# Moving the first chunk of x from TensorE transposes to a VectorE transpose through memory, with a later `fade` and new orders

## The chip, the cores and the metric

One of the cores of a Trainium2 chip runs the whole program. The time is the device time of one execution in microseconds, given as the median of several runs.

## The reference, cut to what matters

One layer works on an input of 2 sequences of 512 tokens and 512 channels: a layer norm, a state-space scan with a convolution, gates and a grouped norm, a product back to 512 channels, and then a feed-forward block with low-rank additions. What the change touches is the scan and the data it reads.

```python
proj = input_states @ in_proj_w.T             # gate, xBC, dt
xBC = silu(causal_conv(xBC, taps=4) + conv_b)  # x: 128 heads x 64; B, C: 8 groups x 128
cum = cumsum(dt * A)                           # within a chunk
scores = (C @ B.T) * exp(cum_i - cum_j), masked to j <= i
y_intra = scores @ (dt * x)                    # inside a chunk
state   = exp(cum_last) * state + B.T @ (dt * exp(cum_last - cum) * x)
y_inter = (C * exp(cum)) @ state_before        # across chunks
y = y_intra + y_inter + D * x
g = rmsnorm_by_group(y * silu(gate)) * norm_w
out = x_in + g @ out_w.T                       # then the feed-forward block
```

The result does not depend on the length of a chunk; the kernel uses chunks of 128 tokens.

## The kernel before

**Tiling.** The 128 heads come in 8 groups of 16 heads. A group has 1024 channels of x (8 tiles of 128) and one tile each of B and C. Each of the 2 sequences has `SC` = 4 chunks of 128 tokens, so that a group has 8 slots, `k` = 0 to 7, with `b = k // 4` the sequence and `c = k % 4` the place in it. `K = 8 g + k` numbers all 64 slots. All products are made with fp32 values split into a high and a low part (`_h`, `_l`): three matmuls for one product.

**What a slot does.** While slot `k` works on its chunk, the projections of the unit after it (group and sequence) run between: 18 weight tiles, 5 in each of the first three slots of a sequence and 3 in the last one (`SLOT_TILES`). Tile names are `g` for a gate tile and `c` for a convolved tile. PE's order in a slot is: `inside` (line 1899, the chunk's own scores times `xdt`), `square_total` (1976), `new_state` (lines 1821 to 1823 on `xw_h`, `xw_l`, `b_tok_h`, `b_tok_l`), one tile, `turn_x` (1873) where the next chunk is turned on PE, `match` (1882, 1883) and `across` (1914) of the next chunk, and the rest of the tiles with the two halves of the out-projection (`out_half`, lines 1960, 1943, 1950) between them. In a sequence's last slot there is no `new_state` and no `across`.

**Turning x.** The convolved x lies with channels on partitions (`x_ch`), and `xdt` and `xw` need tokens there. For `c` = 0, and for the first three slots of all, PE does eight 128x128 transposes into the banks `xt`, from which DVE multiplies by dt (`scale_x`, line 1481). For the other chunks DVE transposes blocks of 32x32 (`turn_x`, line 1503) into a staging buffer, SP stores that in four pieces to memory (`store_x`, line 530), fetches it back as rows (`fetch_x`, line 540, into `x_rows`), and DVE scales it from there (line 1490). `x_sq_of` and `on_pe` say which chunk goes which way.

**The other engines' steps.** DVE adds the skip term (`add_skip`, 1533), moves or adds the new state (`add_state`, 1572 and 1570), reads the mean square (1578), multiplies by the gate (`gated`, 1546), adds to the output (`accumulate`, 1584), decays the state (`fade`, 1555), convolves (`taps`, 1458), scales `across` (1522), makes the low part of the output weights (`ow_low`, 1464, in a group's first slot) and multiplies the scores (`scores`, 1512). POOL makes the low parts of the weights (`w_low`, 771), masks (`mask`, 777), makes `xw` (`weigh_x`, 796) and `xw_l` (`xw_low`, 804) and `gT_l` (`gT_low`, 811), and sums squares (817 to 821). ACT makes the high parts, drains banks and takes the exponentials (1026). `inside` needs `xdt_ready` and the slot's scores, `new_state` needs `xw_l`.

**Buffers share memory.** `under` places a name on the memory of the next one. `x_rows` lies on `gT_l`, `xw` and `xw_sq` on `xw_l`, `ec_sq` on `ec`. So `gT_low` of a slot has to wait until `scale_x` of the next chunk has read `x_rows`.

**What sets the order.** Each engine runs its own list of instructions in the order written out by hand in `body(g, last)`, once for every engine, and waits on semaphores. All DMAs go through one queue, issued by SP in its written order; a wait on SP holds every DMA behind it.

## Time and profile before

| what | value |
|---|---|
| median of 3 runs | 1715.68 us (1715.34 to 1719.24) |
| profiled execution | 1716.82 us, its span 1715.0 us |
| PE busy | 1696.1 us, 99% |
| DVE, POOL, ACT busy | 1298.6, 1229.7, 1194.9 us |
| granted TensorE clock | 0.999 of full speed |
| `turn_x` on PE, line 1873 | 144 transposes, 14.4 us busy |
| fetches of x, line 540 | 46 of 512 KB |

The groups 1 to 6 repeat each other: PE's idle time before a group's first slot's fifth tile, for one, comes every 184.8 us. So one boundary between two groups, from 614 to 662 us, is read in detail. A timeline merges equal instructions that follow each other; a busy time in it is that of the merged row. A matmul of 512 columns starts 0.23 us after the one before it, although its row says 0.39: they overlap.

### The profile page before, as it was taken

The page shows a single profiled execution, that of the slowest core. Times are in us where ns is not written, and L with a number is a line of the kernel's source. Part 1 is how long each engine was busy: PE and PEld are TensorE (multiplying, and loading weights), DVE is VectorE, ACT ScalarE, POOL GpSimd, SP SyncE. Part 2 cuts the span into 40 slices and gives each one's busy share as a digit, 9 for nine tenths or more (in the row PEclk, how much of TensorE's full clock was granted, in tenths as well). Part 3 has the DMA queues.
Part 4 walks back from the last instruction along what each step waited for, and adds up shares of the span by engine and source line. Part 5 has one row for each costly group of instructions (what it writes and reads, how often), then busy time and mean ns, then how long its engine had stood idle before and what let it go on. Part 6 is the DMA issues. An engine that isn't in the chain of part 4 may idle for free.

```text
span 1715.0 us, 27399 instructions
## 1 busy us (share of the span) xinstructions
PE 1696.1 (99%) x9557; PEld 1406.3 (82%) x9557; DVE 1298.6 (76%) x2200; ACT 1194.9 (70%) x2232; POOL 1229.7 (72%) x1058
## 2 busy tenths in 40 slices
PE   9999999999999999999999999999999999999999
PEld 7788888888888888888888888888888888787887
DVE  8897778868796879787986889687977799664323
ACT  6877677777877787777777777768777777663411
POOL 5586778787787778787877788777878687774610
PEclk9999999999999999999999999999999999999999
DMA  5654547464665555555746465556555564554301
GB/s 188 175 137 140 166 145 214 118 172 134 201 166 152 160 170 159 151 155 148 213 131 168 117 203 163 152 164 184 164 147 148 154 201 117 164 137 136 86 10 49
DMA packets 155176, 259.86 MB, mean 152 GB/s; under 512 B 27936, under 2 KB 56224, under 8 KB 155040
## 3 DMA queue, kind: packets, MB, share of 16 engines
q1 hardware_dynamic: 155040, 258.11, 52.4%
q8 instruction: 77, 1.26, 0.3%
q14 instruction: 59, 0.48, 0.1%
HBM read 229.21 MB, written 28.84 MB: 150 GB/s over the span
## 4 chain that ended last, share of the span: by engine, by line
PE 90%; DVE 5%; POOL 1%; issue 1%; DMA 1%; ACT 1%; SPq 0%; DVEq 0%; ACTq 0%; POOLq 0%
PE bank L1821 18%; PE bank L1823 17%; PE bank L1822 17%; PE bank L1899 7%; PE bank L1960 6%; PE bank L1943 6%; PE bank L1950 6%; PE bank L1914 4%; DVE ow_l L1464 2%; PE bank L2204 1%; PE bank L2206 1%; PE bank L2205 1%; PE bank L1976 1%; DVE bcT L1458 1%; PE bank L1883 1%
## 5 line engine op out<-in xcount | busy, mean ns | idle before, releaser
L771 POOL TENSOR_TENSOR w_l<-w_raw,w_h 128x512 fp32r<-128x512 f32 x288 | 397.6, 1383 | 270.2 <-ACT w_h L973 269.9
L1821 PE MATMUL bank<-x_h,w_h 128*128 128x512 f32 (+1 forms) x1328 | 527.1, 397 | 10.0 <-DVE bcT L1458 5.9
L1823 PE MATMUL bank<-x_h,w_l 128*128 128x512 f32 (+1 forms) x1328 | 519.1, 391 | 0.0
L1822 PE MATMUL bank<-x_l,w_h 128*128 128x512 f32 (+1 forms) x1328 | 518.1, 390 | 0.0
L1026 ACT ACTIVATE decay<-decay,cols 128x128 f32<-128x128 f32 x1024 | 318.3, 390 | 3.6 <-POOL decay L777 1.5
L1458 DVE SCALAR_TENSOR_TENSOR x_ch<-bank,par,x_ch 128x511 f32<-128x511 f32 (+2 forms) x384 | 286.3, 746 | 34.2 <-ACT x_ch L991 25.0
L1821 PEld LDWEIGHTS bank<-x_h,w_h 128*128 128x128 f32 (+1 forms) x1328 | 249.6, 188 | 64.1 <-issue 11.7
L1823 PEld LDWEIGHTS bank<-x_h,w_l 128*128 128x128 f32 (+1 forms) x1328 | 249.1, 188 | 54.0
L1822 PEld LDWEIGHTS bank<-x_l,w_h 128*128 128x128 f32 (+1 forms) x1328 | 249.8, 188 | 50.5
L777 POOL TENSOR_SCALAR_AFFINE_SELECT decay<-decay 128x512 f32<-128x512 f32 x256 | 200.7, 801 | 69.6 <-DMA decay<-cum_scratch 68.6
L1512 DVE TENSOR_TENSOR decay<-decay,bank 128x512 f32<-128x512 f32 x256 | 171.0, 682 | 81.6 <-ACT decay L1026 81.4
L991 ACT ACTIVATE x_ch<-bank,par 128x512 f32<-128x512 f32 x128 | 98.9, 773 | 154.6 <-PE bank L1823 154.6
L1533 DVE SCALAR_TENSOR_TENSOR bank<-x_ch,par,bank 128x128 f32<-128x128 f32 x512 | 138.3, 349 | 81.7 <-PE bank L1899 81.7
L973 ACT ACTIVATE w_h<-w_raw 128x512 fp32r<-128x512 f32 x288 | 178.9, 622 | 15.2 <-DMA w_raw<-in_wp 15.1
L811 POOL TENSOR_TENSOR gT_l<-sgT,gT_h 128x1024 fp32r<-128x1024 f32 x64 | 154.1, 2407 | 8.4 <-DVE xdt L1490 7.6
L1012 ACT ACTIVATE sgT<-bank 128x512 f32<-128x512 f32 x122 | 71.8, 590 | 102.9 <-PE bank L1823 102.7
L1960 PE MATMUL bank<-ow_h,gT_h 128*128 128x512 f32 x512 | 137.3, 390 | 0.0
L1943 PE MATMUL bank<-ow_l,gT_h 128*128 128x512 f32 x512 | 136.9, 389 | 0.0
L1950 PE MATMUL bank<-ow_h,gT_l 128*128 128x512 f32 x512 | 136.8, 389 | 0.0
L1899 PEld LDWEIGHTS bank<-decay,xdt 128*64 128x64 f32 x2048 | 110.5, 137 | 22.6 <-issue 22.6
L1899 PE MATMUL bank<-decay,xdt 128*64 128x128 f32 x2048 | 125.9, 276 | 0.0
L804 POOL TENSOR_TENSOR xw_l<-xw,xw_h 128x1024 fp32r<-128x1024 f32 x48 | 115.0, 2396 | 0.3 <-ACT xw_h L1038 0.3
(164 smaller groups left out, 2775.8 us busy)
## 6 DMA issues: line engine op xcount, KB each, us to landing
w_raw<-in_wp SPq DMA_DIRECT2D x288, 256.0 KB, 3.6
decay<-cum_scratch SPq DMA_DIRECT2D x256, 256.0 KB, 4.7
ec<-ecum_scratch SPq DMA_DIRECT2D x96, 256.0 KB, 7.0
x_rows<-xt_scratch SPq DMA_DIRECT2D x46, 512.0 KB, 3.3
ow_raw<-in_ow SPq DMA_DIRECT2D x64, 256.0 KB, 5.4
xt_scratch<-xw_sq SPq DMA_DIRECT2D x124, 128.0 KB, 3.0
w_raw<-in_w SPq DMA_DIRECT2D x48, 256.0 KB, 2.8
xt_scratch<-ec_sq SPq DMA_DIRECT2D x60, 128.0 KB, 2.4
```

Of the source, the lines that this page charges most:

```text
L771: pool.tensor_tensor(w_l[:, s, :], w_raw[:, s, :], w_h[:, s, :].bitcast(F32), ALU.subtract).then_inc(wl_ready, 1)
L777: pool.affine_select(out=d, in_=d, compare_op=ALU.is_ge, fill=fill, base=0, pattern=[[0, QH], [1, P]], channel_multiplier=-1).then_inc(mas ...
L973: act.activation(w_h[:, s, :], w_raw[:, s, :], ACT.Copy).then_inc(wh_ready, 1)
L1026: last = act.activation(decay[:, h, :], decay[:, h, :], ACT.Exp, bias=cols[:, b, CUM, c, h:h + 1], scale=-1.0)
L1458: dve.scalar_tensor_tensor(out=conv(bu, t)[:, s:], in0=bank_of(u, i)[:, 0:SEQ - s], scalar=w, in1=conv(bu, t)[:, s:], op0=ALU.mult, op1=AL ...
L1821: pe.matmul(dst, wh, xh, start=(opens and k == 0), stop=False)
L1822: pe.matmul(dst, wh, xl, start=False, stop=False)
L1823: last = pe.matmul(dst, wl, xh, start=False, stop=(k == len(terms) - 1 and not more))
L1899: last = pe.matmul(yb[n // 4][a * HDIM:(a + 1) * HDIM, tok(n % 4)], xdt[:, h * HDIM:(h + 1) * HDIM], decay[:, h, :], start=(c == 0), stop= ...
L1943: last = pe.matmul(ob[:, :], gT_h[:, n, :], ow_l[:, n, :], start=False, stop=(k == 0 and n == CT - 1))
L1950: last = pe.matmul(ob[:, :], gT_l[:, n, :], ow_h[:, n, :], start=False, stop=(k > 0 and n == CT - 1))
L1960: pe.matmul(ob[:, :], gT_h[:, n, :], ow_h[:, n, :], start=(n == 0), stop=False)
```

## The change

What it does, engine by engine:

- All first chunks but the very first (`K` = 4, 8, ..., 60; 15 of them) are turned by DVE into `gT_sq`, a new name on the memory of `gT_l`, stored, and fetched into `xw`. PE's `turn_x` remains for `K` = 0, 1, 2. Chunks `c` = 2 are staged in `xh_sq`, a new name on `xw_h`. The scratch memory and its semaphores become four (`SC`) in place of two, and the counts in `moved_no` and `stored_no` follow.
- DVE, last slot of a sequence: `turn_x` of the next first chunk directly behind `add_skip`; `accumulate`, `turn_x` of its second chunk and three of the four `scores` ahead of `scale_x`.
- DVE, first slot of a sequence: `mean_square` and `gated` ahead of `add_state`. First slot of a group: `fade` behind the taps of its third tile.
- PE, first slot of a sequence (but the very first): its first tile ahead of `new_state`, its second behind.
- SP, last slot: `store_x` and `fetch_x` of the first chunk ahead of the store of the third.
- POOL, last slot: `gT_low` waits for the store of the first chunk; `square_sum` ahead of `weigh_x`.
- ACT, last slot: all exponentials and both remaining tiles ahead of `xw_high`; in a sequence's first slot `xw_high` waits for the store out of `xh_sq`.
- The last group's second sequence gets matching orders, and a few waits of PE name other semaphores (left out below).

```diff
@@ -461,19 +463,19 @@
-            return ec_sq if k % SC == 1 else xw_sq
+            return (gT_sq, ec_sq, xh_sq, xw_sq)[k % SC]
+
+        def rows_at(k):
+
+            return xw if k % SC == 0 else x_rows
         def on_pe(K):
-            return K % SC == 0 or K < SC - 1
-
-        def pe_no(K):
-
-            return K + 1 if K < SC - 1 else SC - 1 + K // SC
+            return K < SC - 1
         def moved_no(K):
-            return 1 if K < SC else (SC - 1) * (K // SC - 1) + K % SC + 1
+            return K - SC + 2
...
@@ -525,19 +527,20 @@
                 sp.wait_ge(x_turned, turned_no(K))
-                dst = xt_dram[K % 2].rearrange("(b t) (c f) -> c t b f", b=QUADS, c=QUADS)
+                dst = xt_dram[K % SC].rearrange("(b t) (c f) -> c t b f", b=QUADS, c=QUADS)
                 for q in range(QUADS):
                     sp.dma_start(dst[q], x_sq_of(k)[q * SQ:(q + 1) * SQ, :, :, :].rearrange("p b n t -> p b (n t)")
-                                 ).then_inc(x_stored[K % 2], 16)
+                                 ).then_inc(x_stored[K % SC], 16)
             def fetch_x(g, k):
                 K = g * CHUNKS + k
                 if on_pe(K):
                     return
-                sp.wait_ge(x_stored[K % 2], stored_no(K))
-                sp.wait_ge(out_done, 2 * (K - 1))
-                sp.dma_start(x_rows[:, :], xt_dram[K % 2]).then_inc(x_fetched, 16)
+                sp.wait_ge(x_stored[K % SC], stored_no(K))
+                if k % SC > 0:
+                    sp.wait_ge(out_done, 2 * (K - 1))
+                sp.dma_start(rows_at(k)[:, :], xt_dram[K % SC]).then_inc(x_fetched, 16)
...
@@ -717,6 +720,8 @@
                     if c == SC - 1:
+                        store_x(gn, kn)
+                        fetch_x(gn, kn)
                         store_x(gn, kn + 2)
...
@@ -790,9 +795,7 @@
                 if c == 2:
-                    pool.wait_ge(x_stored[1], stored_no(K + 1))
-                elif c == 0 and some(K):
-                    pool.wait_ge(x_stored[0], stored_no(K + 2))
+                    pool.wait_ge(x_stored[SC - 1], stored_no(K + 1))
                 pool.tensor_tensor(per_head(xw[:, :]), per_head(xdt[:, :]), spread(cols[:, b, ELAST, c, :], HDIM),
...
@@ -806,7 +809,9 @@
                 pool.wait_ge(gTh_ready, K + 1)
-                if not on_pe(K + 1):
+                if c == SC - 1 and K < GROUPS * CHUNKS - 1:
+                    pool.wait_ge(x_stored[0], stored_no(K + 1))
+                elif K < GROUPS * CHUNKS - 1 and not on_pe(K + 1):
                     pool.wait_ge(xdt_ready, K + 2)
...
@@ -937,8 +942,11 @@
                         norm_inverse(1, 1)
+                    if c == SC - 1:
+                        square_sum(g, k)
                     weigh_x(gn, kn)
-                    square_sum(g, k)
+                    if c < SC - 1:
+                        square_sum(g, k)
                     if c == SC - 1:
...
@@ -1035,6 +1043,9 @@
                 act.wait_ge(xw_ready, n_state(g, k) + 1)
+                K = g * CHUNKS + k
+                if k % SC == 0 and some(K):
+                    act.wait_ge(x_stored[2], stored_no(K + 2))
                 act.activation(xw_h[:, :], xw[:, :], ACT.Copy).then_inc(xw_h_ready, 1)
...
@@ -1272,13 +1283,11 @@
                         for q in range(QUARTERS):
-                            if q == QUARTERS - 1 and not last:
-                                xw_high(gn, kn)
                             exps(gn, kn, q)
                         if last:
-                            xw_high(gn, kn)
                             norm_high(1, 2)
                         tile(tiles[1:-1] if last else tiles[1:])
+                        xw_high(gn, kn)
                         if k == CHUNKS - 1:
...
@@ -1494,6 +1503,8 @@
                 dve.wait_ge(silu_done, conv_no(2 * g + b, CONV_TILES))
+                if c == 0:
+                    dve.wait_ge(out_done, 2 * (K - 1))
                 if c == 1:
...
@@ -1662,9 +1673,9 @@
                     add_skip(LAST, k)
-                    add_state(LAST, k)
                     norm_apply(1, k - 1)
                     gated(LAST, k)
+                    add_state(LAST, k)
                     norm_low(1, k - 1)
...
@@ -1730,10 +1741,16 @@
                     add_skip(g, k)
+                    if c == SC - 1:
+                        turn_x(gn, kn)
                     if first:
                         gated(g, k)
                         add_state(g, k)
                         taps_of(tiles[2:3])
+                    elif c == 0:
+                        mean_square(*before)
+                        gated(g, k)
+                        add_state(g, k)
                     else:
...
@@ -1761,11 +1778,14 @@
                             ow_low(g, j)
+                    if c == SC - 1:
+                        accumulate(*before)
+                        turn_x(gn, kn + 1)
+                        for q in range(QUARTERS - 1):
+                            scores(gn, kn, q)
                     scale_x(gn, kn)
-                    if not first:
+                    if not first and c < SC - 1:
                         accumulate(*before)
-                    if c == SC - 1:
-                        turn_x(gn, kn + 1)
                     if k == 0:
...
@@ -1775,21 +1795,23 @@
                     taps_of(tiles[1:2])
-                    if k == 0 and not first:
-                        fade(gn, kn)
                     if k > 0:
                         scale_across(gn, kn)
-                        scores(gn, kn, 0)
-                        scores(gn, kn, 1)
+                        if c < SC - 1:
+                            scores(gn, kn, 0)
+                            scores(gn, kn, 1)
                     if not first:
                         taps_of(tiles[2:3])
                     if k == 0:
+                        if not first:
+                            fade(gn, kn)
                         scale_across(gn, kn)
                         for j in range(OW_EARLY + 2, CT):
                             ow_low(g, j)
                         scores(gn, kn, 0)
                         scores(gn, kn, 1)
-                    scores(gn, kn, 2)
+                    if c < SC - 1:
+                        scores(gn, kn, 2)
                     if k == 0:
...
@@ -2076,9 +2096,10 @@
                     square_total(LAST, k - 1)
+                if k == SC:
+                    project(LAST, 1, TILES - 1)
                 new_state(LAST, k)
                 if k == SC:
-                    project(LAST, 1, TILES - 1)
                     match(LAST, k + 1)
...
@@ -2140,10 +2161,15 @@
                         square_total(*((g, k - 1) if k else (g - 1, CHUNKS - 1)))
+                    late_state = c == 0 and not first
+                    if late_state:
+                        projects(tiles[:1])
                     new_state(g, k)
                     if first:
                         projects(tiles[3:4])
-                    if not first:
+                    if late_state:
+                        projects(tiles[1:2])
+                    elif not first:
                         if last and c == SC - 1:
...
@@ -2167,7 +2192,7 @@
                     if not first:
-                        projects(tiles[1:3])
+                        projects(tiles[2 if c == 0 else 1:3])
                     out_half(g, k, 0)
```

## Rows read from the trace of the kernel before

**Rows 1.** Page, first part: busy time of every engine, share of the span.

```profile
PE 1696.1 (99%) x9557; PEld 1406.3 (82%) x9557; DVE 1298.6 (76%) x2200; ACT 1194.9 (70%) x2232; POOL 1229.7 (72%) x1058
```

**Rows 2.** Waits of PE: waiting line, releaser: us in total, times, longest.

```profile
PE bank L1821 <- DVE bcT L1458: 5.9, 7, 0.9
```

**Rows 3.** Timeline (start us, us, operation, [idle before]): PE, sequence's last slot, transposes.

```profile
619.66 0.40 PE L1823 MATMUL bank<-x_h,w_l 128*128 128x512 f32 x1
619.89 0.80 PE L1873 MATMUL bank<-ident_r,x_chr 128*128 128x128 f32 x8
620.53 0.25 PE L1882 MATMUL bank<-ident_r,bcTr 128*128 128x128 f32 x1
```

**Rows 4.** Timeline of PE: out-projection of that slot, then the group's first slot.

```profile
626.39 1.07 PE L1960 MATMUL bank<-ow_h,gT_h 128*128 128x512 f32 x4
...
631.92 1.97 PE L1899 MATMUL bank<-decay,xdt 128*64 128x128 f32 x32
...
634.06 0.48 PE L1821 MATMUL bank<-xw_h,b_tok_h 128*128 128x512 f32 x1
...
652.25 0.47 PE L1821 MATMUL bank<-x_h,w_h 128*128 128x512 f32 x1 [0.80 <-DVE bcT L1458]
...
660.05 0.48 PE L1821 MATMUL bank<-xw_h,b_tok_h 128*128 128x512 f32 x1
```

**Rows 5.** Timeline of SP: the four stores of a chunk of `x` in that slot.

```profile
620.71 1.76 SPq L530 DMA_DIRECT2D xt_scratch<-xw_sq  x4
```

**Rows 6.** Source view of line 530, the stores: issue to landing.

```profile
DMA to landing us min/median/max: 2.0/2.9/5.5
```

**Rows 7.** Source view of line 540, the fetches: issue to landing.

```profile
DMA to landing us min/median/max: 3.1/3.3/6.8
```

**Rows 8.** Timeline of POOL over both slots.

```profile
624.26 2.41 POOL L811 TENSOR_TENSOR gT_l<-sgT,gT_h 128x1024 fp32r<-128x1024 f32 x1
626.63 1.91 POOL L796 TENSOR_TENSOR xw<-xdt,cols 128x1024 f32<-128x1024 f32 x1
...
633.43 2.56 POOL L771 TENSOR_TENSOR w_l<-w_raw,w_h 128x512 fp32r<-128x512 f32 x2
639.67 1.28 POOL L771 TENSOR_TENSOR w_l<-w_raw,w_h 128x512 fp32r<-128x512 f32 x1 [3.68 <-ACT w_h L973]
...
642.24 2.40 POOL L811 TENSOR_TENSOR gT_l<-sgT,gT_h 128x1024 fp32r<-128x1024 f32 x1 [0.34 <-DVE xdt L1490]
644.59 4.21 POOL L777 TENSOR_SCALAR_AFFINE_SELECT decay<-decay 128x512 f32<-128x512 f32 x4
...
657.39 2.38 POOL L804 TENSOR_TENSOR xw_l<-xw,xw_h 128x1024 fp32r<-128x1024 f32 x1
```

**Rows 9.** Timeline of DVE over both slots.

```profile
616.04 2.16 DVE L1533 SCALAR_TENSOR_TENSOR bank<-x_ch,par,bank 128x128 f32<-128x128 f32 x8 [2.75 <-PE bank L1899]
...
628.24 0.69 DVE L1512 TENSOR_TENSOR decay<-decay,bank 128x512 f32<-128x512 f32 x1 [0.49 <-ACT decay L1026]
...
635.74 1.29 DVE L1572 COPY state<-bank 128x512 f32<-128x512 f32 x2 [0.51 <-PE bank L1823]
637.01 1.28 DVE L1546 TENSOR_TENSOR sgT<-bank,sgT 128x512 f32<-128x512 f32 x2
638.20 1.41 DVE L1464 SCALAR_TENSOR_TENSOR ow_l<-ow_raw,par,ow_h 128x512 fp32r<-128x512 f32 x2
640.05 2.05 DVE L1490 TENSOR_TENSOR xdt<-x_rows,cols 128x512 f32<-128x512 f32 x2 [0.44 <-DMA x_rows<-xt_scratch]
642.68 5.63 DVE L1464 SCALAR_TENSOR_TENSOR ow_l<-ow_raw,par,ow_h 128x512 fp32r<-128x512 f32 x4
648.23 1.65 DVE L1555 TENSOR_TENSOR state<-state,cdec 128x1024 f32<-128x1024 f32 x1
649.80 2.31 DVE L1458 SCALAR_TENSOR_TENSOR bcT<-bank,par,bcT 128x511 f32<-128x511 f32 x3
...
655.97 2.47 DVE L1512 TENSOR_TENSOR decay<-decay,bank 128x512 f32<-128x512 f32 x4
```

More of the change, by code:

```diff
@@ L131, in build @@
     cols_dram = nc.dram_tensor("cols_scratch", (GROUPS, BATCH, P, UNIT_COLS), F32, kind="Internal").ap()
-    xt_dram = nc.dram_tensor("xt_scratch", (2, P, GCH), F32, kind="Internal").ap()
+    xt_dram = nc.dram_tensor("xt_scratch", (SC, P, GCH), F32, kind="Internal").ap()
     cdec_dram = nc.dram_tensor("cdec_scratch", (BATCH, GROUPS, GH * SC), F32, kind="Internal").ap()
@@ L180, in build @@
         xdt = sc("xdt", [P, GCH])
+        xh_sq = under("xh_sq", [P, QUADS, CT, SQ])
         xw_h = sc("xw_h", [P, GCH], F32R)
@@ L189, in build @@
         x_rows = under("x_rows", [P, GCH])
+        gT_sq = under("gT_sq", [P, QUADS, CT, SQ])
         gT_l = sc("gT_l", [P, CT, P], F32R)
@@ L334, in build @@
         x_turned = sem("x_turned")
-        x_stored = [sem(f"x_stored{n}") for n in range(2)]
+        x_stored = [sem(f"x_stored{n}") for n in range(SC)]
         x_fetched = sem("x_fetched")
@@ L482, in stored_no @@
         def stored_no(K):
-            return 16 * QUADS * (K // 2 if K % 2 else K // SC)
+            return 16 * QUADS * (K + 1) // SC if K % SC == SC - 1 else 16 * QUADS * (K // SC)
         @block.sync
@@ L1471, in scale_x @@
                 if on_pe(K):
-                    dve.wait_ge(tx_done, pe_no(K))
+                    dve.wait_ge(tx_done, K + 1)
                 else:
@@ L1484, in scale_x @@
                     return
-                xs = x_rows.rearrange("p (a s n t) -> p a n s t", a=2, s=QUADS // 2, n=CT)
+                xs = rows_at(k).rearrange("p (a s n t) -> p a n s t", a=2, s=QUADS // 2, n=CT)
                 xd = xdt.rearrange("p (n a s t) -> p a n s t", n=CT, a=2, s=QUADS // 2)
@@ L1830, in norm_transpose @@
                 if k == 1 and c == 2:
-                    pe.wait_ge(xdt_ready, (GROUPS - 1) * CHUNKS + SC + 1)
+                    pe.wait_ge(x_l_ready, CHUNKS + 1)
                 if k == 1 and c in (SC, SC + 1):
@@ L1866, in turn_x @@
                     pe.wait_ge(silu_done, conv_no(2 * g + b, CONV_TILES))
-                if K == MIDDLE + 1:
-                    pe.wait_ge(x_l_ready, CHUNKS + 2)
                 if some(K):
@@ L1974, in square_total @@
                 if K == MIDDLE:
-                    pe.wait_ge(xdt_ready, K + 2)
+                    pe.wait_ge(x_l_ready, CHUNKS + 2)
                 pe.matmul(total_of(K), y[:, 0, :], ones[:, :], start=True, stop=True).then_inc(ss_done, 1)
@@ L2153, in body @@
                         projects(tiles[1:-1])
-                        turn_x(gn, kn)
                     else:
```

## Prediction

> **What bounds the kernel now.** I read the busy times first. PE is busy for 1696.1 us of a span of 1715.0 [rows 1], so only two things move the time: work taken from PE, and waits given to it. The waits of PE come next. The only one that repeats is 5.9 us in 7 pieces, PE behind the taps of the tile `bcT` [rows 2], once in each group's first slot (groups 1 to 7). The timeline of one boundary between groups then shows how near the other engines are to PE. In the group's first slot DVE has work in every microsecond from 640.05 to the last scores at 658.4 [rows 9], and POOL's last piece, `xw_l`, ends at 659.77 [rows 8] for a `new_state` at 660.05 [rows 4]. That is 0.28 us to spare on POOL. So this slot is bound by three engines at once, while a sequence's last slot is bound by PE alone.
>
> **Eight transposes go, 15 times.** Without them the product `match` would start where the first transpose starts: 620.53 - 619.89 = 0.64 us [rows 3]. 15 x 0.64 = 9.6 us off PE. For the boundary into the last group's second sequence I count it separately below; 14 x 0.64 = 9.0 us for the others. This step is sure, as nothing else runs on PE in that time.
>
> **What replaces them in the last slot.** DVE transposes when `add_skip` ends, at 618.20 [rows 9]. SP now issues its first store of this slot at 620.71, as soon as DVE has turned that chunk [rows 5]; the new chunk is turned earlier, and I take 620.45 for its first store. The fourth is issued 1.3 us later and lands 2.9 us after that [rows 6]: 624.7. Two things hang on it.
> First, `gT_l`. POOL started it at 624.26 [rows 8]; it would start at 624.7 and end at 627.1. The out-projection starts 0.64 us earlier than 626.39 [rows 4], and its third set of four matmuls (0.91 us a set, four starts 0.23 apart as in [rows 3]) needs `gT_l` at 625.75 + 1.81 = 627.56. Cover 0.45 us, cost nothing; with a landing at the longest 5.5 us [rows 6] it would cost 2.1.
> Second, the fetch: 624.75 + 3.3 [rows 7] = 628.1. `scale_x` now stands behind the third `scores`, which ends at 628.93 [rows 9], so the fetch is hidden by 0.8 us. Two instructions of 1.03 us as in the row at 640.05 [rows 9] end at 631.0. PE wants `xdt` at 631.92 - 0.64 = 631.28 [rows 4]. It fits by 0.3 us. SP is blocked from 622.2 to 624.7; the weight load, two sets of stores and the next unit's loads are behind it. They come up to 3 us later, the weights a tile or more ahead of need: nothing counted.
> `xw` then runs 631.0 to 632.9 (1.91, [rows 8]), ACT's copy an estimated 1.1 more (under half of POOL's 2.4 for the same tile) to 634.0, `xw_l` 2.4 more to 636.4. `new_state` now stands behind a tile of 12 matmuls, 2.81 us, so PE comes to it at 631.28 + 2.14 + 2.81 = 636.2 and waits 0.2. At the 7 boundaries inside groups 0 to 6 that is all: 7 x 0.2 = +1.4 us; bounds 0 and, with the scaling or the copy a slot of work late, 1 us each.
>
> **What it does in a group's first slot (7 times).** I measure from the start of `inside` (631.92 before). `new_state` moves from 2.14 to 5.15, 3.0 us later, and with it `add_state` on DVE from 3.82 to 6.85 [rows 4, 9]. `mean_square` and `gated` (1.3 us) go into the gap, yet DVE then has nothing to do from about 4.65 to 6.85. `add_state` ends at 8.1 where the queue before reached the first `ow_l` at 6.28.
> Now POOL is in the way. DVE instructions with both tensors in SBUF and POOL's instructions exclude each other in this trace: four `ow_l` take 5.63 us and four masks 4.21 us side by side, against 1.41 us for two `ow_l` while POOL rests, and `gT_l` keeps its 2.40 [rows 8, 9]. After the change POOL has `xw_l` until 5.1, two `w_l` until 7.65 and the third until 8.95 (1.28 each, [rows 8]), so the first `ow_l` waits to 8.95, and `scale_x` ends at about 11.7 in place of 642.10 - 631.92 = 10.2. `gT_l` waits for it: start 11.8 in place of 10.32.
> From there to the end of `xw_l` POOL took 659.77 - 642.24 = 17.5 us [rows 8], with nothing of it idle but for DVE's turns. The order behind is the same but for `fade`, which now meets `weigh_x` and the sums in place of a mask's end; I take 17.5 to 18.1. `xw_l` ends at 29.3 to 29.9, and `new_state` of the next slot starts at 29.4 to 30.0 against 28.1 [rows 4]: +1.3 to +1.9, I take 1.8, as `fade`'s own 1.1 us no longer overlaps a mask.
> DVE alone says less: scores start 1.6 to 2.0 us after 24.05 [rows 9], the last of them ends near 28.2, `inside` cannot end before 28.6 and `new_state` not start before 28.9, +0.7. The larger wins.
> And the wait on the taps: `fade` leaves their front (1.6 us), but `add_state`, the turns with POOL and `scale_x` put 1.5 us there. The taps end about where they did, 20.1. The 5.9 us of [rows 2] are not earned, and this is already in the +1.8, which is measured past it. 7 x 1.8 = +12.6 us; bounds: 0 (everything absorbed) and 2.3 (a late `x_rows` besides, whose fetch has one more set of stores ahead of it).
>
> **Where it costs nothing.** In the second sequence's first slot there are no `ow_l`, and DVE and POOL both have microseconds to spare; the later `add_state` still ends a microsecond ahead of `across`. The last group's boundary has `norm_apply` behind `scale_x` on DVE and a transposition of PE behind that; the fetch's 3.3 us [rows 7] stand ahead of it with few scores to hide them. Bounds -0.6 and +3; I take +1.
>
> **Sum:** -9.0 + 1.4 + 12.6 + 1.0 = +6.0 us. On the profile's span 1715.0 -> 1721.0; the profiled execution took 1716.8, the median of the runs is 1715.7, and on that I forecast 1721.7 us.
>
> **The skill against the trace.** Eight transposes of 128x128 cost PE 0.64 us here, 0.08 each [rows 3]. The Trainium skill, "VectorE: DVE Perf Modes", section "The three transpose paths", prices a 128x128 transpose on TensorE at 390 ns, and its "Rules for kernel authors" say to use TensorE for it where PSUM will do, which speaks against this change; by its price the removal would be an estimated 15 x 8 x 0.39 = 47 us. The trace has the duration, so 9.6 stands.
> That the first `ow_l` beside `gT_l` waits for all of it is seen in the 5.63 us [rows 9]. The skill's "SBUF — State Buffer", section "Who interferes with whom", says that a DVE instruction with two SBUF inputs and a POOL instruction that reads SBUF lock each other out for the whole instruction. The trace agrees, and without such locking the same work would cost the slot an estimated 1 us less.
>
> **The rivals.**
> (1) *The relief works.* If DVE and POOL keep up in a group's first slot (the third `w_l` comes earlier or `ow_l` gets its turn between), the wait of [rows 2] goes and nothing replaces it: 1715.7 - 9.6 - 5.9 = 1700.2. It decides at `gT_l`: if it starts by 10.3 after `inside`, this is the case. For it: 9.6 us are sure. Against it: `add_state` is 3.0 us later by PE's own order, on an engine without idle time. With half of that it ends at 1700 to 1709.
> (2) *Even.* The slot loses only what DVE alone gives, 0.7, or up to 1.2: 1715.7 - 9.0 + 1.4 + 1.0 + 7 x 0.7 (1.2) = 1714.0 (1717.5); with absorbed small terms 1709 to 1717.
> (3) *The detour through memory is late.* If stores and fetch land 2 to 3 us later than the medians (the longest are 5.5 and 6.8 [rows 6, 7]), `inside` waits for `xdt` at every boundary, since its cover is 0.3 us plus 0.8: 14 x 1 to 2 us on top of the forecast, 1736 to 1750. Against it: the fetch starts on a queue just emptied by the wait for the stores.
>
> **How the numbers follow.** Within 0.3% is 5.1 us, about what a measurement of this kernel can tell from no change: 1710.5 to 1720.9. The forecast and its neighbourhood (1717 to 1730) has 0.45, of which 0.1 lies under 1720.9; rival 2 has 0.23, of which 0.20 is "same" and 0.03 faster; rival 1 has 0.17, nearly all faster; rival 3 has 0.15. Faster 0.19, same 0.30, slower 0.51. The range leaves out the better half of rival 1 and the upper part of rival 3: 1707 to 1734.
>
> **What would show it.** Right: no transposes on 1873 beyond 24; about 15 x 0.64 less PE time; DVE idle for about 2 us ahead of the copy into `state` (1572) in first slots; `gT_l` in a group's first slot starting more than 11 us after `inside`; a new wait of PE on `xw_l` (POOL, line 804) or on the scores in the slot behind, near 1 us each time. Wrong: PE's waits in total under 15 us with `gT_l` at 10.3; or PE waiting for `xdt` (line 1490) in `inside`, which would be rival 3.

## Result and the profile after

The changed kernel takes 1728.77 us (median of 4 runs, 1726.24 to 1729.52) against 1715.61 for the kernel before beside it: 13.2 us more; the ratio on record is 1.0064, 95% interval 1.0052 to 1.0076. It is slower by 0.6 to 0.8%. The profiled executions have spans of 1727.7 and 1715.0 us, 12.65 apart. The granted TensorE clock was 0.998 of full speed in the longer one and 0.999 in the other; where it fell in the longer one is looked at under the run late. First the busy times of the kernel after, as [rows 1]:

```profile
PE 1698.5 (98%) x9437; PEld 1393.3 (81%) x9437; DVE 1324.3 (77%) x2215; ACT 1196.3 (69%) x2232; POOL 1243.1 (72%) x1058
```

PE has 120 instructions less (15 x 8 transposes), and yet 2.4 us more busy time, and 10 us more of its span are idle. (With the transposes alone gone, in the run cut below, PE's busy time falls by 9.7 us, to 1686.4.) What it now waits for (waiting line, releaser: us in total, times, longest), as [rows 2]:

```profile
PE bank L1963 <- DVE ow_l L1473: 3.8, 7, 0.6
PE bank L1843 <- DVE x_ch L1467: 3.4, 2, 2.5
PE bank L1861 <- DVE sgT L1381: 3.2, 1, 3.2
PE bank L1970 <- POOL gT_l L816: 2.9, 6, 1.2
PE bank L1843 <- issue: 2.8, 8, 0.4
...
PE bank L1843 <- DVE bcT L1467: 0.6, 2, 0.4
```

The 5.9 us behind the taps of [rows 2] are down to 0.6. In their place stand `ow_l` (7 times, once in each group's first slot), `gT_l` (in last slots), one wait of 3.2 us in the last group, and 2.8 us in 8 pieces that the profile puts down to "issue". Seven of these eight are `new_state` in the slot behind a group's first one. It starts 0.10 us after `xw_l` ends in all seven, so what it waits for is `xw_l`. An ended wait is not a gain: the same slots got longer.

**Where the time went.** I measured every slot as the distance between two starts of `inside` (PE, line 1919 of the kernel after, 1899 before, as in [rows 4]) and took the differences. With 0.03 us in the other slots they make the whole 12.65 us:

| slots | forecast | after | what it is |
|---|---|---|---|
| 14 last slots of a sequence, groups 0 to 6 | -9.0 | -3.8 | transposes gone, `gT_l` late |
| 7 first slots of a second sequence | +1.4 | +2.5 | `new_state` behind a late `xw_l` |
| 7 first slots of a group, and the slot behind each | +12.6 | +3.2 and +6.2 | `gT_l` late, and by it `xw_l` for the slot behind |
| last group's boundary, two slots | +1.0 | +4.25 | `norm_apply` behind `scale_x`, and a lower clock behind that wait |
| start-up to the first `inside` | 0 | +0.4 | 81.1 to 84.4 us over the profiled executions here |
| sum | +6.0 | +12.6 | |

The boundary of [rows 4] in the kernel after, timeline of PE (start us, us, operation, [idle before]):

```profile
622.90 0.40 PE L1845 MATMUL bank<-x_h,w_l 128*128 128x512 f32 x1
623.13 0.22 PE L1902 MATMUL bank<-ident_r,bcTr 128*128 128x128 f32 x1
...
629.84 1.07 PE L1963 MATMUL bank<-ow_l,gT_h 128*128 128x512 f32 x4
631.03 1.20 PE L1970 MATMUL bank<-ow_h,gT_l 128*128 128x512 f32 x4
...
634.88 1.97 PE L1919 MATMUL bank<-decay,xdt 128*64 128x128 f32 x32
...
640.12 0.47 PE L1843 MATMUL bank<-xw_h,b_tok_h 128*128 128x512 f32 x1
...
660.16 1.20 PE L1963 MATMUL bank<-ow_l,gT_h 128*128 128x512 f32 x4 [0.58 <-DVE ow_l L1473]
661.29 2.11 PE L1919 MATMUL bank<-decay,xdt 128*64 128x128 f32 x32
...
664.10 0.47 PE L1843 MATMUL bank<-xw_h,b_tok_h 128*128 128x512 f32 x1 [0.39 <-issue]
```

The transpose of `match` (1902) starts 0.23 us behind the tile's last matmul: the 0.64 us of [rows 3] are gone. But the set on `gT_l` (1970) starts 1.19 us behind the set before it, where a set takes 0.91. The group's first slot is 661.29 - 634.88 = 26.41 us long (25.99 before), and `new_state` of the slot behind starts 29.22 us after `inside` (28.13 before).

SP, POOL and DVE in the same stretch, as [rows 5], [rows 8] and [rows 9]:

```profile
623.71 2.76 SPq L532 DMA_DIRECT2D xt_scratch<-gT_sq  x4
628.44 0.34 SPq L543 DMA_DIRECT2D xw<-xt_scratch  x1
```

```profile
628.56 2.41 POOL L816 TENSOR_TENSOR gT_l<-sgT,gT_h 128x1024 fp32r<-128x1024 f32 x1 [1.03 <-DMA xt_scratch<-gT_sq]
630.92 1.30 POOL L822 TENSOR_TENSOR y<-y 128x512 f32<-128x512 f32 x1
...
637.60 2.41 POOL L807 TENSOR_TENSOR xw_l<-xw,xw_h 128x1024 fp32r<-128x1024 f32 x1 [1.17 <-ACT xw_h L1049]
639.96 3.81 POOL L776 TENSOR_TENSOR w_l<-w_raw,w_h 128x512 fp32r<-128x512 f32 x3
643.71 1.02 POOL L831 TENSOR_TENSOR rstd<-mean_sq,minus_half 128x1 f32<-128x1 f32 x1
646.33 2.40 POOL L816 TENSOR_TENSOR gT_l<-sgT,gT_h 128x1024 fp32r<-128x1024 f32 x1 [1.59 <-DVE xdt L1499]
...
661.64 2.36 POOL L807 TENSOR_TENSOR xw_l<-xw,xw_h 128x1024 fp32r<-128x1024 f32 x1
```

```profile
641.78 1.29 DVE L1583 COPY state<-bank 128x512 f32<-128x512 f32 x2 [2.21 <-PE bank L1845]
642.99 1.99 DVE L1473 SCALAR_TENSOR_TENSOR ow_l<-ow_raw,par,ow_h 128x512 fp32r<-128x512 f32 x2
644.90 1.28 DVE L1499 TENSOR_TENSOR xdt<-x_rows,cols 128x512 f32<-128x512 f32 x2
...
654.53 2.56 DVE L1566 TENSOR_TENSOR state<-state,cdec 128x1024 f32<-128x1024 f32 x1
```

Read them from `inside` at 634.88. In the last slot, `gT_l` waits 1.03 us for the fourth store to land. In the group's first slot `xw_l` ends at 5.1, three `w_l` at 8.9, the first two `ow_l` at 10.1, `xdt` at 11.3, and `gT_l` starts at 11.45; before it started at 10.32 [rows 8]. `fade` (line 1566) takes 2.56 us where it took 1.65 [rows 9].

### The profile page after: what moved, and what is told of

The parts are those of the page before. It is cut to its first block, busy times and chain, and to the rows that moved or that the text cites. A ratio compares the mean times of both kernels' runs of the same rounds, so it can differ in the third digit from the quotient of the medians.

```text
span 1727.7 us, 27263 instructions
## 1 busy us (share of the span) xinstructions
PE 1698.5 (98%) x9437; PEld 1393.3 (81%) x9437; DVE 1324.3 (77%) x2215; ACT 1196.3 (69%) x2232; POOL 1243.1 (72%) x1058
## 4 chain that ended last, share of the span: by engine, by line
PE 84%; DVE 8%; DMA 3%; SPq 2%; issue 1%; POOL 1%; ACT 1%; DVEq 0%; POOLq 0%
PE bank L1843 17%; PE bank L1845 16%; PE bank L1844 16%; PE bank L1919 7%; PE bank L1970 6%; PE bank L1963 6%; PE bank L1980 6%; PE bank L1934 4%; DVE ow_l L1473 3%; DMA xt_scratch<-gT_sq 2%; PE bank L2230 1%; PE bank L2231 1%; PE bank L2229 1%; SPq L532 1%; PE bank L1996 1%
## 5 line engine op out<-in xcount | busy, mean ns | idle before, releaser
L1963 PEld LDWEIGHTS bank<-ow_l,gT_h 128*128 128x128 f32 x512 | 96.1, 189 | 26.7 <-DVE ow_l L1473 6.8
```

The costliest lines, as they stand in the source:

```text
L1963: last = pe.matmul(ob[:, :], gT_h[:, n, :], ow_l[:, n, :], start=False, stop=(k == 0 and n == CT - 1))
```

## Experiments

Each kernel was timed beside the kernel before; "group pair" below is the sum of a group's first slot and the one behind it, over 7 groups, against the kernel before. The changed kernel has +9.4 there.

**What eight transposes cost: run cut.** The kernel before, without PE's transposes of the later first chunks:

```diff
                         projects(tiles[1:-1])
-                        turn_x(gn, kn)
 ...
-                        if on_pe(gn * CHUNKS + kn):
+                        if gn * CHUNKS + kn < SC - 1:
                             turn_x(gn, kn)
```

> The kernel before without PE's 15 turns of a sequence's first chunk; DVE scales what lies in the banks, so that chunk's x is left out of the computation. Nothing else is moved. Theory A (the transposes were worth 0.64 us each on PE): 15 x 0.64 = 9.6 us less, 1706.0 us. Rival R1 (the removal itself gives less, as PE then waits for something else in the last slots, and the changed kernel's last slots show just that): 3 to 5 us less, 1711 to 1713 us.

Measured: 1709.78 us, ratio 0.9957 [0.9943, 0.9971]. The 14 last slots are 0.70 us shorter each (-9.8), and the slot behind each is 0.21 longer (+3.0). The first number is a little over the 0.64 of [rows 3]; the second I had not counted. It lies ahead of that slot's own `new_state`, whose `xw_l` is made around the end of the last slot. POOL before, then POOL and PE of the run cut (its `inside` at 627.76):

```profile
631.10 2.39 POOL L804 TENSOR_TENSOR xw_l<-xw,xw_h 128x1024 fp32r<-128x1024 f32 x1
```

```profile
627.65 2.37 POOL L804 TENSOR_TENSOR xw_l<-xw,xw_h 128x1024 fp32r<-128x1024 f32 x1
```

```profile
630.12 0.47 PE L1821 MATMUL bank<-xw_h,b_tok_h 128*128 128x512 f32 x1
```

Before, this `xw_l` ends at 633.49 and `new_state` starts at 634.06 [rows 4], 0.57 us later. In the run cut `new_state` starts 0.10 us behind `xw_l`, and 2.35 us behind `inside` in place of 2.14: PE comes 0.70 us earlier and finds only 0.47 of it free. (The 0.28 us of the prediction's first paragraph belong to another `xw_l`, the one for the slot behind.) The kernel leaves out the x of these chunks, so it only tells times. Removal by itself is worth 7 us, so everything else in the change had to cost less than that.

**The later `fade` alone: run fade.** The kernel before with one line moved:

```diff
-                    if k == 0 and not first:
-                        fade(gn, kn)
 ...
                     if k == 0:
+                        if not first:
+                            fade(gn, kn)
                         scale_across(gn, kn)
```

> The kernel before with only the later fade in the groups' first slots. Theory A (that slot is bound by POOL's chain to xw_l too, which had 0.28 us to spare): PE's wait on the taps goes, and a wait on xw_l takes most of its place; 7 x 0.3 us = 2 us less, 1713.6 us, or nothing. Rival (the taps were the only bound): 5.9 us less, 1709.8 us.

Measured: 1718.78 us, ratio 1.0010 [1.0001, 1.0020]. The first slots are 0.68 us shorter each (-4.8), the slots behind them 0.80 to 1.4 longer (+6.5), so +0.24 a group. Theory A has the mechanism and a wrong size, its rival missed. The timelines of POOL and of DVE, `inside` at 632.41:

```profile
650.52 1.90 POOL L796 TENSOR_TENSOR xw<-xdt,cols 128x1024 f32<-128x1024 f32 x1
652.39 2.29 POOL L817 TENSOR_TENSOR y<-y 128x512 f32<-128x512 f32 x1
```

```profile
650.95 2.56 DVE L1555 TENSOR_TENSOR state<-state,cdec 128x1024 f32<-128x1024 f32 x1
```

`fade` starts while POOL has `xw`, ends 1.1 us behind it, and POOL's next piece (817) takes 2.29 where it took 1.30 at the same place before. But before, `fade` cost POOL the same microsecond at another piece, a `w_l` of 2.26 us in place of 1.3. So POOL's chain to the next slot's `xw_l` comes out as long as it was: that `xw_l` ends 28.0 to 28.15 us after `inside` (27.9 before), and in six of the seven groups `new_state` starts 0.10 us behind it. POOL before; then POOL and PE of the run fade in a group of the usual kind (`inside` at 817.84):

```profile
648.77 2.26 POOL L771 TENSOR_TENSOR w_l<-w_raw,w_h 128x512 fp32r<-128x512 f32 x1
```

```profile
843.54 2.37 POOL L804 TENSOR_TENSOR xw_l<-xw,xw_h 128x1024 fp32r<-128x1024 f32 x1
```

```profile
846.01 0.47 PE L1821 MATMUL bank<-xw_h,b_tok_h 128*128 128x512 f32 x1 [0.38 <-issue]
```

The wait of PE has only gone from the taps to `xw_l` in the next slot. (In the seventh group, the one of the first two timelines, PE waits 0.46 us for scores inside `inside`.)

**The first slot's orders without the detour: run first.** The run fade's edit, and `add_state` and `new_state` late as in the change; the chunk stays on PE:

```diff
+                    elif c == 0:
+                        mean_square(*before)
+                        gated(g, k)
+                        add_state(g, k)
 ...
+                    late_state = c == 0 and not first
+                    if late_state:
+                        projects(tiles[:1])
                     new_state(g, k)
```

> The kernel before, PE's transposes kept, with the first slots' new orders alone: new_state behind a tile, mean_square and gated ahead of add_state, later fade. Theory A (these orders cost the groups' first slots their time, by making DVE idle until the late state): the slots 0 and 1 of the groups lose together about 1.0 to 1.3 us as in the changed kernel, 7 to 9 us in all, 1723 to 1725 us. Rival R2 (the loss comes from the detour of x through memory and its traffic, which this kernel does not have): within 2 us of before.

Measured: 1718.73 us, ratio 1.0013 [1.0003, 1.0022]. Group pair +2.4, of which the run fade has +1.7. `gT_l` starts at 10.51 in all 7 groups, 0.14 later than before. So the late `add_state`, to which I had given a part of the 12.6 us, costs about 0.1 us a group as long as `x` comes from PE. DVE's idle time ahead of it is there, 1.85 us in each group, and it costs almost nothing.

**The fourth store: run state.** The changed kernel, with the new chunk staged in memory that lies under `state`, so that `gT_l` has no store to wait for:

```diff
-            return (gT_sq, ec_sq, xh_sq, xw_sq)[k % SC]
+            return (st_sq, ec_sq, xh_sq, xw_sq)[k % SC]
 ...
-                if c == SC - 1 and K < GROUPS * CHUNKS - 1:
-                    pool.wait_ge(x_stored[0], stored_no(K + 1))
```

> The changed kernel with the first chunks staged on the memory of the scan's state, which is dead in a last slot, so that gT_low waits for no store; add_state waits for it instead, long after. Theory A: the last slots get back what PE waited for gT_l, 14 x 0.37 = 5.2 us, and some of the last group's boundary: 1723 us. Rival R2 (the traffic delays other things as well, so that the wait for gT_l is replaced by one for xdt): 1727 to 1729 us.

Measured: 1723.18 us, ratio 1.0036 [1.0022, 1.0049]. The 14 last slots sum to -9.2, against -3.8 in the changed kernel; PE's wait on `gT_l` is gone. This settles the 5.4 us. Waits of POOL in the changed kernel, and the landing of these stores (tile view of `gT_sq`):

```profile
POOL gT_l L816 <- DMA xt_scratch<-gT_sq: 16.2, 15, 2.2
```

```profile
DMA to landing us min/median/max: 2.0/3.0/4.4
```

The median is what I had used (2.9, [rows 6]), and for the fourth store alone it is 2.9 too (2.4 to 3.5, once 4.4). The cover was 0.45 us, and in these 14 slots the fourth store landed 9.85 to 11.44 us after `inside` (mean 10.3) against a forecast of 9.8. Most of that is its issue: I had it at 6.85 us after `inside`, SP issued it at 7.0 to 7.1 in ten slots and at 7.8 to 8.0 in four, as at 623.71 above, where four issues take 2.76 us. What holds these four back stays open.

**The last group's boundary: run late.**

```diff
-                        scale_x(gn, kn)
                         norm_apply(1, 2)
+                        scale_x(gn, kn)
```

> The changed kernel with one exchange on DVE in the last group's boundary: norm_apply of the third chunk stands ahead of scale_x. Theory: PE's wait of 3.2 us for sgT (the product of norm_apply, which stands behind the fetch of x) is what made this boundary 4 us longer; with the exchange the wait goes and xdt comes at most 0.7 us later, behind three quarters of a microsecond of work that has to be done anyway: 1728.8 - 3 = 1725.8 (1725 to 1726.5), and the boundary's slot is within 2 us of the kernel before. Rival: inside of the next slot needs xdt and scores just as late as norm_apply's product, so the wait only moves to inside: 1728 to 1729. Everything else is as in the changed kernel in both.

Measured: 1727.39 us, ratio 1.0052 [1.0037, 1.0067]. The boundary falls from +4.25 to +2.3, but it is +3.0 in four other kernels that leave it as in the change (state, refade, gap and behind). In the changed kernel, DVE, then PE, then the windows view of all engines behind PE's wait:

```profile
1467.46 2.41 DVE L1499 TENSOR_TENSOR xdt<-xw,cols 128x512 f32<-128x512 f32 x2 [1.41 <-DMA xw<-xt_scratch]
1469.80 0.67 DVE L1381 TENSOR_SCALAR sgT<-acc,moments,inv_std 128x512 f32<-128x512 f32 x1
```

```profile
1470.52 0.75 PE L1861 MATMUL bank<-ident_r,sgT_r 128*128 128x128 f32 x4 [3.24 <-DVE sgT L1381]
...
1471.48 2.05 PE L1980 MATMUL bank<-ow_h,gT_h 128*128 128x512 f32 x4
...
1476.88 1.97 PE L1919 MATMUL bank<-decay,xdt 128*64 128x128 f32 x32
```

```profile
1470.10:1476.90 6.80, 6.38 (x20) 4.76 (x20) 3.62 (x8) 5.88 (x11) 4.50 (x5) 0.50 0.97 276
```

The number behind the engines' busy times is the granted clock: 0.50, that is 1.2 GHz in place of 2.4, for 6.8 us from 1470.1, which is 2.8 us into PE's wait. The three sets of the out-projection half between the last two rows of PE take 5.40 us. The same half takes 2.92 in the kernel before, where the clock is 1.00 over the whole boundary and PE waits at most 0.9 us at a time. So 2.5 of the 4.25 us are the clock. In the four other kernels the clock is 0.50 for 3.4 us, behind the same wait (3.1 to 3.3 us), and this half takes 4.51 to 4.53: 1.6 of their 3.0. The prediction has no term for the clock.

With the exchange PE's wait on `sgT` is 1.1 us, but a wait of 0.9 for `y` follows it, and the clock is 0.50 for 3.4 us all the same; the half takes 4.34. So against the four kernels of the same 3.4 us the exchange gains 0.7 us of the 3 that I expected.

**`fade` back at its old place: run refade.** The run fade's edit, undone in the changed kernel.

> The changed kernel with fade back ahead of the taps of the third tile in a group's first slot. Theory A, from the run of the later fade alone (+0.25 a group: -0.68 in the group's first slot and +0.85 in the one behind): it adds to the detour's loss and is independent of it: the first slot gets 0.6 longer, the one behind loses its +0.85, in all 7 x 0.25 = 1.7 us less, 1727.0. Rival B: the late xdt is what delays the slot behind, not fade: then only the wait for the taps comes back (0.84 x 7), and the time is 1731 to 1734. Rival C: fade meets no POOL instruction at its old place and gives its whole 0.9 back with nothing lost: 1722 to 1724.

Measured: 1727.90 us, ratio 1.0061 [1.0037, 1.0085]. Group pair +7.9 in place of +9.4: the first slots rise to +8.0, the slots behind fall to -0.1. The wait on the taps is back, and larger than the 5.9 of [rows 2] (waits of PE, run refade):

```profile
PE bank L1843 <- DVE bcT L1467: 11.3, 7, 1.7
```

Theory A holds to 0.2 us. It also shows the rest by itself: without the later `fade` the loss of a group is 7.9 / 7 = 1.13 us, and `gT_l` starts 1.10 us later than before (11.47 against 10.37, medians of the 7 groups). The delay of `gT_l` passes one to one into the time of these two slots. The four executions lie between 1725.06 and 1733.06, at clocks from 0.999 down to 0.995, so this reading rests on the slots and not on the median.

**Why `gT_l` is late: runs gap and behind.** The run gap puts the first two `ow_l` into DVE's idle time; the run behind takes one `w_l` of POOL out of the way and puts it behind `gT_l`:

```diff
                         gated(g, k)
+                        if k == 0:
+                            for j in range(OW_EARLY // 2):
+                                ow_low(g, j)
                         add_state(g, k)
```

```diff
+                    late_w = k == 0 and some(g * CHUNKS)
+                    if not late_w:
+                        lows(tiles[:1])
 ...
                     gT_low(g, k)
+                    if late_w:
+                        lows(tiles[:1])
```

> The changed kernel with the first two ow_l of a group's first slot in DVE's idle 2.2 us, ahead of add_state. Theory P (the port shared with POOL is the bound from the end of xw_l on): after xw_l ends at 5.14 behind the start of inside, three w_l (3.8), two ow_l (1.4) and scale_x (1.3) take turns with nothing idle between, so scale_x ends near 11.3 to 11.7 whatever their order, and gT_l starts no earlier than 11.3: time 1728 to 1730. Theory D (DVE's own idle time ahead of add_state is the loss, as the forecast had it): scale_x ends 0.9 to 1.4 earlier, gT_l starts at 10.1 to 10.5, and 7 x 0.7 to 1.0 come back: 1722 to 1724.

> The changed kernel with POOL's first w_l of a group's first slot moved behind gT_l (into the time when POOL works and DVE has its ow_l). Theory P: POOL's last w_l ahead of the first ow_l ends at 7.6 instead of 8.9, the two ow_l take 1.4 in place of 2.0, scale_x ends at 10.7 in place of 11.3 and gT_l starts at 10.85 in place of 11.45. Its masks then come 0.7 later, so the total moves little: 1726 to 1730; what tells is gT_l. Theory D: gT_l stays at 11.3 or later, as the end of add_state sets it, and everything behind is 1.3 later: 1733 or more.

Measured, gap: 1726.36 us, ratio 1.0050 [1.0034, 1.0067]. Group pair +8.35, `gT_l` at 11.22 (median); the time lies between what the two theories gave. The profiled execution is 4.4 us shorter than that of the changed kernel, but only 1.0 of it is the group pair; 1.1 are the last slots, 1.2 the last boundary (the clock, above), 0.7 the second sequence's first slots, 0.4 the start-up. Measured, behind: 1732.06 us, ratio 1.0081 [1.0066, 1.0096]. Group pair +13.6, `gT_l` at 10.85. POOL and then DVE of the run gap (`inside` at 632.62), then POOL of the run behind (`inside` at 635.83):

```profile
635.31 2.41 POOL L807 TENSOR_TENSOR xw_l<-xw,xw_h 128x1024 fp32r<-128x1024 f32 x1 [1.17 <-ACT xw_h L1049]
637.67 5.24 POOL L776 TENSOR_TENSOR w_l<-w_raw,w_h 128x512 fp32r<-128x512 f32 x3
...
643.85 2.39 POOL L816 TENSOR_TENSOR gT_l<-sgT,gT_h 128x1024 fp32r<-128x1024 f32 x1
```

```profile
637.38 2.60 DVE L1473 SCALAR_TENSOR_TENSOR ow_l<-ow_raw,par,ow_h 128x512 fp32r<-128x512 f32 x2
```

```profile
640.74 2.55 POOL L776 TENSOR_TENSOR w_l<-w_raw,w_h 128x512 fp32r<-128x512 f32 x2
...
646.50 2.39 POOL L816 TENSOR_TENSOR gT_l<-sgT,gT_h 128x1024 fp32r<-128x1024 f32 x1 [2.71 <-DVE xdt L1503]
648.86 1.75 POOL L776 TENSOR_TENSOR w_l<-w_raw,w_h 128x512 fp32r<-128x512 f32 x1
```

DVE started its two `ow_l` 3.4 us earlier than in the changed kernel (4.8 for 8.1 behind `inside`), and `gT_l` came 0.2 earlier. Two `ow_l` took 2.60 us in place of 1.99 in the changed kernel (1.41 in [rows 9]), three `w_l` 5.24 in place of 3.81: each engine pays for the other, and with little idle time left the order of these pieces hardly matters. Take one piece of 1.28 us out, and `gT_l` starts 0.6 earlier, as expected (10.85, the very number). That speaks for theory P: from the end of `xw_l` the two engines together have 3.8 + 1.4 + 1.3 = 6.5 us of work that excludes each other, and 5.1 + 6.5 = 11.6, where `xdt` was ready at 11.3 in the changed kernel. But the piece that was moved comes back behind `gT_l`: the time 1732.06 lies above the 1726 to 1730 that I gave, as 0.48 (`gT_l`) + 1.28 (the `w_l`) + 0.24 (`fade`) = 2.0 us a group, and 13.6 / 7 = 1.94 were measured. I had the sum's parts and not the sum.

The page "SBUF — State Buffer" of the Trainium skill, in "Who interferes with whom", has this exclusion, for instructions of DVE with two SBUF inputs beside instructions of POOL that read SBUF; the 2.60 and 5.24 us of the run gap agree.

**All four remedies together: run all4.** State, late, refade and gap in one.

> The changed kernel with four edits together: staging of the first chunk in the memory under state (run state), norm_apply ahead of scale_x in the last group (run late), fade back at its old place (run refade), ow_l in DVE's idle time (run gap). If the four causes are independent, their gains over the changed kernel's span of 1727.7 add up: 7.6 - 0.4 + 2.0 + 1.5 + 1.7 = 12.4, so a span near 1715.3 and a time of 1716 (1714.5 to 1718), that is no difference from the kernel before. If the port between DVE and POOL is the one cause under state, refade and gap, they overlap and the span stays at 1718 or more.

Measured: 1719.90 us (12 runs, 1714.57 to 1724.20), ratio 1.0015 [1.0007, 1.0024]. The gains don't add up: the group pair is +7.9, as in refade alone, so gap brings nothing more once `fade` is back. The span of the profiled execution is 1721.3, of which 1.3 is a longer start-up; so the second of the two cases came, the one of overlapping gains.

**Only the second sequence's chunk: runs half and half2.** In half a group's first chunk stays on PE with all the orders of before, and the second sequence's first chunk goes the new way, staged as in the run state. In half2 the last group's boundary is as before too:

```diff
         def on_pe(K):
-            return K < SC - 1
+            return K < SC - 1 or K % CHUNKS == 0 or K == MIDDLE + 1
```

(and in all queues `k == SC - 1` where the change has `c == SC - 1`, `k == SC` where it has `c == 0`; without `K == MIDDLE + 1` it is the run half, with `norm_apply` first.)

> Only the second sequence's first chunk goes by DVE and memory (staged under state, norm_apply first in the last group); the next group's first chunk stays on PE with all the orders of before at that boundary and in the group's first slot. Theory: the loss of the detour sits in the first slot of a group, where POOL's xw_l comes 2.4 us into a port that is full; in the second sequence's first slot there is no ow_l, so it costs 0.25 to 0.45 there. Sum against before: 7 x (-0.7 + 0.35) + 1.0 (last boundary, with the exchange) = -1.5, so 1714.1 (1712 to 1715.5), all in slots 3 and 4 of the groups, and slots 0 and 1 as before to 0.1 us. Rival: the late orders of the second sequence's first slot cost as much as a group's first one (1.3 each): 1719 to 1722.

> As the run half, but the last group's boundary is also as before (its first chunk on PE, orders of before). Theory: what is left is 7 last slots at -0.70 each and 7 slots behind them at +0.27 to 0.70, so slots 3 and 4 sum to -2 to -2.5, the last group's boundary is as before to 0.1 us, and the time is 2 us under the kernel before of this run (ratio 0.9988), if start-up falls alike. Rival: the last boundary's loss in half came from the detour of the groups before (a late queue carried over), then slots 3 and 4 of the last group still lose a microsecond and the ratio is 1.000 or more.

Measured, half: 1719.04 us, ratio 1.0015 [1.0007, 1.0024]. The last slots ahead of a second sequence are shorter by 0.70 in all 7 groups (-4.9), their first slots longer by 0.26 to 0.70 (+3.0), the group pair is +0.3. So the loss of 1.3 us a group is gone with the detour in front of it, as the theory said. The time missed it by 5 us: the last group's boundary cost +3.7 instead of +1.0, and start-up of that execution was 1.6 us longer than in the kernel before. Here too the clock is 0.50 for 3.4 us, behind a wait of 1.95 us on `state`; `across` takes 3.62 us there in place of 2.05 before, 1.6 of the 3.7.

Measured, half2: 1714.23 us against 1716.36 beside it, ratio 0.9991 [0.9982, 1.0000] in 11 runs. The slots are -4.9 and +2.4, everything else is within 0.1 us of the kernel before, save for the start-up; the clock is 1.00 over the last group's boundary. This is the only complete version that is not behind the kernel before. Its medians are 2 us lower and its slots 2.5, at the edge of what 11 runs can tell. The waits of PE in it (the taps' wait is that of [rows 2]):

```profile
PE bank L1854 <- DVE bcT L1476: 5.9, 7, 0.9
PE bank L1854 <- DVE x_ch L1476: 2.5, 1, 2.5
```

## Why the prediction was right and wrong

The forecast was 1721.7 us with a range of 1707 to 1734, and slower as the likeliest; 1728.8 came. The direction and the range held; the sum was 6 us where 12.65 were measured. The terms are off on both sides: the last slots by 5.2 us, the last boundary by 3.25 and the second sequence by 1.1 upwards, the groups' first slots by 3.2 downwards. The term that decided for "slower" was this last one. The other errors together are three times as large as its own and of the opposite sign (10 us against 3.2), so that the sum came within 7 us is in part luck.

**Eight transposes, 0.64 us: right.** 0.70 in the run cut. What the step lacked was the return: 0.21 us of each came back in the next slot, since the `xw_l` of that slot's own `new_state` could give only 0.47 us. "Nothing else runs on PE in that time" was true, and did not say what PE would wait for next.

**"Cover 0.45 us, cost nothing": wrong, 5.4 us.** The run state shows that this wait took the last slots from -9.2 to -3.8. The latency that I used was right (2.9 us from issue to landing); the issue was not: the fourth store left 0.15 to 0.2 us later than forecast in ten slots and a microsecond later in four. A cover of 0.45 us took no account of either, nor of the spread of the landings that stood in the same row ([rows 6], 2.0 to 5.5).

**`new_state` in the second sequence's first slot, 0.2 us: a little low,** 0.35 in the changed kernel, 0.35 to 0.43 in half2 and half. It does wait for `xw_l`, which ends at 4.9 to 5.5 in these three; the fetch takes 3.8 us (median) where I took 3.3 from another fetch.

**A group's first slot, 1.8 us: the chain right, one cause and the size wrong.** POOL's pieces fell as forecast (`xw_l` to 5.1, the third `w_l` to 8.9, then `ow_l`), `gT_l` came at 11.45 for 11.8, and from there to the end of `xw_l` it took 17.7 us for my 17.5 to 18.1. Measured were 9.4 / 7 = 1.34 us a group: 1.08 from `gT_l` and 0.24 from `fade`. I took 1.8, near the top of my 1.3 to 1.9, for the fade's own 1.1 us; but POOL pays that microsecond at the old place as well, and the run fade shows `xw_l` 0.15 us later by the move. The role of the late `add_state` was wrong: the run first gives it 0.1 us. What the runs leave as the cause is that `xw_l`, 2.4 us of POOL, now lies 2.7 to 5.1 us after `inside` (-0.8 to 1.6 before), so that POOL's `w_l` come behind it and meet DVE's `ow_l` and `xdt`. The run half, with x of a group's first chunk on PE, has no loss there, and the run behind moves `gT_l` as this reading says; no run moves `xw_l` alone. The prediction had this chain, and put a part of the blame on the idle engine beside it.

**No gain from the taps' wait: right.** It went, and as forecast nothing was earned; the runs fade and refade show where it went, to `xw_l` in front of the next slot's `new_state`. This is the wait that the prediction named as a sign, with 0.4 us a time in place of "near 1". Its other sign, 15 x 0.64 us less PE time, did not come: PE is busy 2.4 us longer.

**The last boundary, +1: too low,** 4.25, and 3.0 in the four other kernels. The fetch, the scaling and `norm_apply` are in a row there with nothing to hide them, and the row of [rows 7] gave the fetch's 3.3 us. But the larger part is a term that the prediction does not have: the granted clock falls to 0.50 behind PE's wait, for 6.8 us (2.5 us of time) in the changed kernel and 3.4 us (1.6) in the four. Without it the boundary costs 1.4 to 1.8, not far from the +1.

**The rivals.** The relief (1700) and the even case (1714 to 1717) did not come. Of the late detour, a part did: not at `inside`, where I looked for it, but at `gT_l`, which waits for the same stores. The sign that I named, PE waiting for `xdt` in `inside`, did not appear.

Still open: in the run half the last group's boundary costs 3.7 us though `norm_apply` stands first, 2.1 of them outside the clock; its waits are on `y`, `sgT` and `state`, and no run takes them apart. No run shows either why the clock stayed low twice as long in the changed kernel's profiled execution, or what its other executions did there; the run all4 has the same 6.8 us. Why the four remedies leave 1.13 us a group, where `gT_l`'s delay of 0.83 would explain less, is not settled either.

## What to carry to other kernels

When work is taken from the bound engine, list for each product it waits for how far ahead of need it lands, and charge every removal against the margin of the first product behind it; here PE could come only 0.47 us earlier out of 0.70, and 0.21 came back. A margin on a DMA is to be held against the spread of its landings and of its issue, not against one row and a median. And where two engines exclude each other, add up their excluding pieces from the last common wait: if that sum fills the time, idle microseconds of one engine are no reserve, and only less work or work at another place helps. When a change makes the bound engine wait for microseconds at a time, look at the granted clock behind the wait.

## What the runs showed of the hardware

Three things I had not expected. The cost of exclusion falls on both engines and depends little on the order: with two pieces started 3.4 us earlier, the run gap gained 0.2. Behind long waits of PE the clock fell. In the last group's boundary it was at 1.2 GHz for 6.8 us in the changed kernel and in all4, and for 3.4 us in state, refade, gap, behind, late and half. PE had waited 3.1 to 3.3 us just before in the changed kernel, state, refade, gap and behind, 1.95 in half, and 1.1 and 0.9 in late, 1.3 and 0.9 in all4. In the five kernels whose longest wait there is 0.9 us (before, cut, fade, first, half2) it stayed at 2.4. Two waits of 1.3 and 0.9 us in half did not bring it down, so the waits alone do not settle it. And the start-up ahead of the first `inside` differs between executions by up to 3 us (81.1 to 84.4 over these kernels), a quarter of the effect studied. Part of that is the clock as well: seven of the thirteen profiled executions have 3.4 us at 1.2 GHz near 60 us and reach `inside` at 82.8 to 84.4, the six others at 81.1 to 83.2. The sums over slots are free of the start-up, while the medians are not.
